# Laying out score operands by DMA instead of by 0/1 matmuls in a four-layer kernel on one Trainium2 core

## What is computed

```python
# layer 0: attention with rotary positions, 16 heads of 8, then a mixture of experts (2 of 8)
# layer 1: attention with a latent of 32 for keys and values, rotary, 16 heads of 8, then a channel mix
# layer 2: attention with sigmoid scores, 16 heads of 8, then a mixture of experts (2 of 8)
# layer 3: linear attention, then an MLP
scores = q @ k.T * 8 ** -0.5          # per head, causal
out = softmax(scores) @ v             # layer 2: sigmoid in place of softmax
```

## Time and profile before

| | |
|---|---|
| runs | 1676.58, 1678.48, 1684.9 us; median 1678.48 us |
| profiled execution | time 1675.6 us, span 1673.8 us from first to last instruction, mean granted TensorE clock 0.925 |
| busy in the span | PE 1430.4 us, DVE 1011.3 us, ACT 726.8 us, POOL 252.6 us |
| stages by the trace | rope attention to about 404 us, routed experts to about 590 us, latent attention to about 984 us, channel mix to about 1045 us, sigmoid attention to about 1272 us, the rest to the end |

### The profile page before, as it was taken

One profiled execution on the slowest core, in us unless ns is written; L12 is line 12 of the kernel. 1 busy time (PEld: TensorE's weight loads), 2 busy tenths in 40 slices (PEclk: granted clock), 3 DMA queues, 4 the chain that ended last, 5 costly groups with the idle time before them and its releaser, 6 DMA issues.

```text
span 1673.8 us, 33692 instructions
## 1 busy us (share of the span) xinstructions
PE 1430.4 (85%) x12538; PEld 1083.1 (65%) x12538; DVE 1011.3 (60%) x2801; ACT 726.8 (43%) x1281; POOL 252.6 (15%) x514
## 2 busy tenths in 40 slices
PE   5999999997069489999999965799996999998987
PEld 3666666664059456666666644466665999997667
DVE  4677777674336347777777649344444666664856
ACT  0444434442246324445444433467664555543322
POOL 0000000000521312222221013000000000001433
PEclk7999999996579769999999979699998999998989
DMA  9100000000022200000000000000000000000001
GB/s 301 31 2 1 1 1 2 2 1 1 34 60 71 96 4 5 8 8 8 8 5 5 2 0 2 1 2 2 2 1 1 1 2 2 1 2 1 1 17 35
DMA packets 32673, 30.39 MB, mean 18 GB/s; under 512 B 4536, under 2 KB 29312, under 8 KB 31872
## 3 DMA queue, kind: packets, MB, share of 16 engines
q1 hardware_dynamic: 30464, 24.05, 4.6%
q0 software_dynamic: 2048, 4.20, 0.8%
HBM read 18.01 MB, written 10.22 MB: 17 GB/s over the span
## 4 chain that ended last, share of the span: by engine, by line
PE 71%; DVE 12%; ACT 5%; issue 4%; POOL 4%; DMA 2%; SPq 0%; POOLq 0%; DVEq 0%; ACTq 0%
PE S L355 12%; PE O L1559 7%; PE O L425 6%; PE S L341 5%; PE A L329 4%; PE S L344 4%; PE A L310 3%; ACT probs L647 3%; PE A L330 3%; PE O L429 3%; PE S L1541 2%; DVE nm L826 2%; PE A L446 2%; PE O L2105 2%; PE S L1542 2%
## 5 line engine op out<-in xcount | busy, mean ns | idle before, releaser
L647 ACT ACTIVATE probs<-S 128x1024 f32<-128x1024 f32 x288 | 289.4, 1025 | 170.3 <-PE S L355 161.7
L823 DVE TENSOR_REDUCE nm<-S 128x4 f32<-128x1024 f32 x128 | 151.7, 1214 | 71.5 <-PE S L355 71.2
L156 POOL TENSOR_TENSOR ve<-mv,eps 128x2 f32<-128x2 f32 x112 | 26.3, 235 | 1075.4 <-DVE mv L148 1075.4
L1627 ACT ACTIVATE probs<-S,eb 128x256 f32<-128x256 f32 x256 | 107.5, 473 | 118.1 <-PE S L1543 118.1
L1559 PE MATMUL O<-ew,probs 128*128 128x128 f32 x1024 | 138.2, 278 | 0.3 <-ACT probs L1627 0.2
L654 ACT COPY OT<-O 128x512 f32<-128x512 f32 x96 | 56.2, 585 | 180.5 <-PE O L429 180.5
L1559 PEld LDWEIGHTS O<-ew,probs 128*128 128x128 f32 x1024 | 125.2, 192 | 5.1 <-ACT probs L1627 3.5
L425 PE MATMUL O<-probs,V 128*32 128x256 f32 x1536 | 123.1, 393 | 4.7 <-ACT probs L647 3.4
L329 PE MATMUL A<-hi,spread 128*128 128x256 f32 x384 | 108.0, 314 | 21.5 <-DVE lo L802 8.8
L167 DVE TENSOR_SCALAR X<-res,mv,rstd 128x128 f32<-128x128 f32 x224 | 85.4, 422 | 66.4 <-POOL rstd L160 65.9
L355 PEld LDWEIGHTS S<-KS,QS 32*128 32x128 f32 x1024 | 74.4, 192 | 57.3 <-issue 57.3
(11 more groups left out here) (341 smaller groups left out, 3065.3 us busy)
## 6 DMA issues: line engine op xcount, KB each, us to landing
ew<-in_w SPq DMA_DIRECT2D x2, 2048.0 KB, 10.2
moe_rows<-zeros SPq DMA_DIRECT2D x1, 2944.0 KB, 13.6
xin<-moe_rows SPq DMA_DIRECT2D x23, 128.0 KB, 2.5
ew<-in_w SPq DMA_DIRECT2D x2, 1024.0 KB
out<-X SPq DMA_DIRECT2D x16, 128.0 KB, 1.8
moe_made<-ctx_sb SPq DMA_DIRECT2D x12, 128.0 KB, 1.8
moe_made<-ctxT SPq DMA_DIRECT2D x11, 128.0 KB, 1.8
probs<-in_spread SPq DMA_DIRECT2D x1, 1024.0 KB, 5.2
```

The costliest lines, as they stand in the source:

```text
L647: act.activation(c.probs[:, n].rearrange("p b g l -> p b (g l)"), c.S[:, n % 2], ACT.Exp if soft else ACT.Tanh, scale=self.scale).then_inc ...
L823: dve.tensor_reduce(c.nm[:, 1, 2 * pr:2 * pr + 2, 2 * u:2 * u + 2], slot.rearrange("p b (g k) -> p b g k", g=2), AX.X, ALU.max, negate=Tru ...
L1627: act.activation(w["h"][:, x % 2, j], c.S[:, x % 2, bank, col:col + L], ACT.Relu, bias=w["b1"][:, x * self.NJ + j:x * self.NJ + j + 1]).th ...
```

## The change

The stacks on PE and both copies are taken out of all three attentions. In their place SP, after a wait for `hi` and then for `lo`, issues 24 DMAs per sequence from SBUF to SBUF, each 32 partitions by 256 numbers (32 KB): channel rows of one group go to every fourth partition of `QS` or `KS`. The strip's row order changes accordingly (`MAX_HI`, `MAX_LO`). Two semaphores, `stk0` and `stk1`, count the landings for groups 0, 1 and groups 2, 3. `QS` is zeroed and `KS` filled with the ones once at the start and once again behind the routed experts, which use the same memory. Weight loads that stood at the start are spread over the steps of the rope and latent attentions, behind the 24 DMAs of a sequence, and the load of `spread` is gone.

```diff
-MAX_HI = 3 * HD
-MAX_LO = MAX_HI + 1
+SLOTS = ROWS // HD
+MAX_HI = SLOTS - 1
+MAX_LO = 2 * SLOTS - 1
...
+    def fill_stacks(self, dve, filled):
+
+        dve.memset(self.QS[:].bitcast(F32), 0.0).then_inc(filled, 1)
+        dve.tensor_copy(self.KS[:].rearrange("p n g l -> p (n g l)"), self.one_rows[:].broadcast_to((P, 2 * G * L))).then_inc(filled, 1)
...
+    def sync(self, sp, others):
+        c, e = self.c, self.e
+        stacks = [c.QS[:].bitcast(F32), c.KS[:].bitcast(F32)]
+        halves = [e["stk0"], e["stk1"]]
+
+        def spread(par, part, j, slot, half):
+            for g in (2 * half, 2 * half + 1):
+                sp.dma_start(stacks[j][slot:P:SLOTS, par, g, :], part[ROWS * g:ROWS * (g + 1), j, :].bitcast(F32))\
+                  .then_inc(halves[half].sem, 16)
+
+        for s in range(B):
+            par = s % 2
+            sp.wait_ge(e["hi"].sem, e["hi"].at(s))
+            if begun(s - 2):
+                sp.wait_ge(e["p2"].sem, e["p2"].at(s - 2))
+            for half in range(2):
+                spread(par, c.hi, 0, 0, half)
+                spread(par, c.hi, 0, 1, half)
+                spread(par, c.hi, 1, 0, half)
+                spread(par, c.hi, 1, 2, half)
+            sp.wait_ge(e["lo"].sem, e["lo"].at(s))
+            for half in range(2):
+                spread(par, c.lo, 0, 2, half)
+                spread(par, c.lo, 1, 1, half)
+            others(s)
...
         def x_transposes(s, par):
-            if begun(s - 1):
-                pe.wait_ge(e["ks"].sem, e["ks"].at(s - 1))
+            if soft:
+                if begun(s - 1):
+                    pe.wait_ge(e["t12"].sem, e["t12"].at(s - 1))
+            elif begun(s - 3):
+                pe.wait_ge(e["ctx"].sem, e["ctx"].at(s - 3))
...
         def pass1(s, par, n):
 
-            if n == 0:
-                pe.wait_ge(e["qs"].sem, e["qs"].at(s))
-                pe.wait_ge(e["ks"].sem, e["ks"].at(s))
             if n < 2:
+                stacked = e["stk1" if n else "stk0"]
+                pe.wait_ge(stacked.sem, stacked.at(s))
...
             pass2(k, par, 3)
-            if has_front:
-                stack(k + 1, 0)
             weighted(k, par, 0, has_front)
             pass2(k, par, 4)
-            if has_front:
-                stack(k + 1, 1)
             pass2(k, par, 5)
...
         def round_hi(s):
             act.wait_ge(e["rot"].sem, e["rot"].at(s))
             if begun(s - 1):
-                act.wait_ge(e["kst_ps"].sem, e["kst_ps"].at(s - 1))
+                act.wait_ge(e["stk0"].sem, e["stk0"].at(s - 1))
+                act.wait_ge(e["stk1"].sem, e["stk1"].at(s - 1))
             act.copy(c.hi[:], c.rot[:]).then_inc(e["hi"].sem, 1)
```

More of the change, by code:

```diff
@@ L391, in pass2 @@
                 pe.wait_ge(e["qm"].sem, e["qm"].at(s, n + 1))
[L392 to L395, removed]
+            if n < 2 and not soft:
+                stacked = e["stk1" if n else "stk0"]
+                pe.wait_ge(stacked.sem, stacked.at(s))
             if n >= 2:
@@ L798, in round_lo @@
             if begun(s - 1):
-                dve.wait_ge(e["kst_ps"].sem, e["kst_ps"].at(s - 1))
+                dve.wait_ge(e["stk0"].sem, e["stk0"].at(s - 1))
+                dve.wait_ge(e["stk1"].sem, e["stk1"].at(s - 1))
             if not soft:
@@ L2227, in dve @@
         finish(self.NT - 1)
+        c.fill_stacks(dve, c.refilled)
         for q in range(self.FIRST):
@@ L2346, in build @@
         load("moe2", second["gate"][:], d["gate_2"])
-        load("moe2", second["w1"], d["w1_2"])
-        load("moe2", second["w2"], d["w2_2"])
+        for k in range(0, NE, 2):
+            load("moe2", second["w1"][:, k:k + 2], d["w1_2"][:, k:k + 2])
+            load("moe2", second["w2"][:, nj2 * k:nj2 * (k + 2)], d["w2_2"][:, nj2 * k:nj2 * (k + 2)])
         load("moe2", second["b1"][:], d["b1_2"])
@@ L2374, in build @@
         rope.after, latent.before = experts0, experts0
-        experts0.loaded = loaded["moe0"], 16 * len(loads["moe0"])
-        N_MADE = 31
+        experts0.loaded = loaded["l0"], 16 * len(loads["l0"])
+        N_MADE = 32
         def fold_products(pe):
@@ L2420, in _, with beside_rope, beside_latent @@
         def _(sp):
-            for group in ("consts", "l0", "x0", "x", "moe0", "l1", "l2", "l3"):
+            for group in ("consts", "l0", "x0", "x"):
                 for dst, src in loads[group]:
                     sp.dma_start(dst, src).then_inc(loaded[group], 16)
-            rows = phases[1][1].rows
             sp.wait_ge(made, N_MADE)
-            sp.dma_start(rows.rearrange("(n p) d -> p n d", p=P),
-                         routed["zeros"][:].unsqueeze(1).broadcast_to((P, rows.shape[0] // P, P))).then_inc(zeroed, 16)
+            rows = phases[1][1].rows.rearrange("(n p) d -> p n d", p=P)
+            early = [(group, *pair) for group in ("moe0", "l1", "l2", "l3") for pair in loads[group]]
+            late = [("moe2", *pair) for pair in loads["moe2"]]
+            def beside_rope(s):
+                for group, dst, src in early[3 * s:3 * s + 3] if s < B - 1 else early[3 * s:]:
+                    sp.dma_start(dst, src).then_inc(loaded[group], 16)
+                if s < ZEROINGS:
+                    n = rows.shape[1] // ZEROINGS
+                    sp.dma_start(rows[:, s * n:(s + 1) * n],
+                                 routed["zeros"][:].unsqueeze(1).broadcast_to((P, n, P))).then_inc(zeroed, 16)
+            def beside_latent(s):
+                for group, dst, src in late[s:s + 1] if s < B - 1 else late[s:]:
+                    sp.dma_start(dst, src).then_inc(loaded[group], 16)
+            rope.sync(sp, beside_rope)
             experts0.sync(sp)
@@ L2430, in _ @@
             sp.wait_ge(experts0.s["bias"], 2 * experts0.NT)
-            for dst, src in loads["moe2"]:
-                sp.dma_start(dst, src).then_inc(loaded["moe2"], 16)
+            sp.wait_ge(c.refilled, 2)
+            latent.sync(sp, beside_latent)
+            phases[4][1].sync(sp, lambda s: None)
             phases[-1][1].sync(sp)
```

66 lines of the change are left out of this document (15 added, 51 removed).

## The result

The changed kernel takes 2149.91 us (median of 4 runs, 2145.45 to 2156.37) against 1679.26 us (4 runs on the same chip, 1676.58 to 1684.9): 1.2801 times as long, 95% interval 1.2770 to 1.2831. The forecast was 1980 us, range 1850 to 2150. The direction was as forecast, and so was the mechanism; the size was 170 us short.

What follows compares the result with a forecast made beforehand. PE's own work was taken to bound the kernel before; DMA waits and clock loss add +113 us in rope, +107 in latent, +72 in sigmoid, which with smaller terms makes +304 on 1675.6: 1980 us, range 1850 to 2150.

Steps and rivals of the forecast that it cites:

- The bound and the way of reading: Attention steps, read in time order: PE-bound before; afterwards score slots wait for DMAs, 11.0 to 12.9 us behind hi.
- Spacing 0.47 us, bounds 0.40 to 0.51: SP's queue behind each hi: time between starts of successive DMA issues, 24 per sequence, taken from loads in the trace.
- Landing 2.0 us: Each new DMA: 2.0 us from the start of its issue until its data has landed in SBUF.
- The clock: PE's clock falls in every stall, returns 4.4 us into `weighted`; costs 2.3 us per rope or latent step, 1.9 in sigmoid.
- clock stays up: Rival: PE's clock does not fall in the stalls, or only now and then; 1876 us, chance 0.17.
- Comes back late: Rival: PE's clock returns only with the projections, 7.2 us lost instead of 2.3 in 32 steps; 2137 us, chance 0.15.
- Last steps, start and gather: Outside the loops: sixteenth sequences' waits +20 us, less loaded at the start -3.4, earlier rows behind routed experts 4.8 saved.
- The transfers hide: Rival: SP's issues cost nothing, only bytes count, so transfers fit beside PE's work; 1569 us, chance 0.05.

Runs made afterwards that it cites:

- hi alone: Changed kernel without the 8 DMAs of the remainders (lo) per sequence, leaving 16: 1895.18 us (one execution).
- five forms: Kernel before, with bursts of 12 unread DMAs on SP in seven forms, varying stride, size and SBUF or HBM as source or destination: 1685.41 us.
- The two queues: Changed kernel with ACT issuing the 8 DMAs of hi into `KS` and SP the other 16: 1947.54 us, 1.1604 times the kernel before.
- the versions through HBM: Changed kernel with hi and lo stored to HBM and loaded back by six or three loads, in several variants: 1831.41, 1790.75, 1800.6 and 1780.43 us.
- the control: Kernel before, stacks by matmul, with only the weight loads spread over the steps and the zeroing in two parts: 1680.4 us, 1.0006.
- direct pairs: Changed kernel with 12 SBUF to SBUF DMAs of 64 KB per sequence (9 SP, 3 POOL), `weighted(k, 1)` moved ahead, 10 filler matmuls: 1718.03 us, 1.0193.
- through HBM, `weighted` first: Changed kernel with hi and lo stored to HBM, six loads back, and `weighted(k, 1)` ahead of `pass1(k+1, 0)` in rope and latent: 1790.75 us, 1.0677.

## Why the prediction was right, and where its size was off

*The bound and the way of reading.* Right: score slots that wait for DMA, with all of the next step queued behind them. hi alone confirms it, since 8 issues taken off the queue gave 4.9 us per step back. The two queues gained as much (5.0 us per rope step), but ended on another path, through ACT's issues and exponentials.

*Spacing 0.47 us, bounds 0.40 to 0.51: the step that failed.* It measured 0.637 on SP, in all five forms from SBUF to SBUF, and 0.66 on ACT, outside the bounds. I took the price from single loads and a group of four, none with this spread of rows. Coming from HBM does not by itself make a load cheaper, since loads from HBM with the change's spread cost 0.64 too. The term of the sum is 23 (or 19) spacings per sequence: 23 x 0.167 = 3.8 us in 32 steps and 19 x 0.167 = 3.2 us in 16, +173 us, and 1980 + 173 = 2153 against 2150 measured. That this closes so well is in part luck, since the errors below cancel, and so is it that 2149.91 lies inside a range that ended at 2150: two of the four executions lie above it, and the room at the top had been left for a clock that comes back late, not for this spacing.

*Landing 2.0 us.* 1.9 measured.

*The clock.* Fall and return as forecast, the return 3.0 instead of 4.4 us into `weighted`. From the second slot to the next hi 17.3 us against 15.4, so 1.9 us per step where 2.3 stood; in sigmoid 6.4 us (1464.22 to 1470.66) against 4.8, 1.6 where 1.9 stood. The rival "clock stays up" did not happen. "Comes back late" happened in one latent step of the changed kernel (5 us, shown above), and in many steps of the versions through HBM.

*Last steps, start and gather.* Outside the three loops the span grew by 31 us; the sum had 12. Most of what was missed lies between the last hi of rope and the first of latent, 237.3 us against 224.4, +13 where the sum had +3. The first hi came 1.8 us earlier (3.4 said). Behind the routed experts the gain was 2.2 us (4.8 said), 4.84 us from 741.84 to 746.68 against the 7.08 of the earlier trace rows; the first of POOL's DMAs took twice as long as usual:
```profile
741.84 1.99 POOL L1926 DMA_INDIRECT yt<-moe_made,sli  x1 [6.44 <-DMA moe_made<-ctx_sb]
...
746.68 0.42 DVE L1943 TENSOR_TENSOR X<-X,yt 128x256 f32<-128x256 f32 x1 [3.72 <-DMA yt<-moe_made,sli]
```
In the control the moved loads gained nothing that could be told from no change. These terms were small and partly wrong, and their errors stand against the lesser clock loss.

*The transfers hide.* Excluded: it needed a spacing of 0.23 us. The run with 12 DMAs shows what it takes, a release by 7.4 us behind hi in every step; it had that in some steps, and over the whole kernel nothing of PE's 99 us was gained.

What stays open: why a wait of 1.11 us leaves the clock up in one kernel and one of 1.12 us is followed by 12 us at 1.2 GHz in another, and whether direct pairs in the old order of `weighted` would beat the kernel before; that was not tried.

## What to carry to other kernels

Count the DMA instructions on a queue before the bytes: here each cost 0.64 us of its engine from 16 to 128 KB, so 24 small ones per step were the critical path with the DMA engines under a quarter busy. A second queue takes its share only by holding up what its engine does behind it. Merge the instructions by laying source and destination out so that one instruction carries more, but check what the merging adds: a round trip through HBM cost two landings, and doubled stores came with full DMA engines. A matmul that only moves data also keeps PE busy; take it away, and a wait that opens in its place can be paid a second time through the clock, 1.9 us per rope step here.

## What the hardware showed that I had not expected

A DMA out of SBUF into SBUF occupied SP for 0.594 us in the median whatever its size between 16 and 128 KB (0.607 for the pairs, 0.619 on ACT, 0.564 on POOL), one to HBM for 0.37 to 0.42. The Trainium skill's advice to coalesce small transfers ("DMA: Bandwidth & Descriptors", section "Rules for kernel authors") agrees: 12 DMAs of 64 KB took 7.5 us of issue (5.82 on SP and 1.70 on POOL, side by side), 24 of 32 KB took 15.2.

POOL's indirect DMA took 1.99 us at 741.84, beside a CAST of 1.16 us on DVE that began at 741.80, and 0.94 to 1.02 elsewhere. In the control with only the moved loads, which has no such CAST there, the same DMA took 1.00. The Trainium skill says in "SBUF — State Buffer", section "SBUF: two separate sides", that GpSimd cannot write descriptors while VectorE runs an operation in a two-port mode, such as a float32 copy from SBUF to SBUF. The two rows agree with that; whether this CAST runs in such a mode no run here shows.

With short waits of PE the granted clock went both ways in the same kernel (through HBM, `weighted` first): steps of 23 and of 31 us stood side by side with the same instructions, about 7 of the 8 us between them made by the clock (20 us at 1.2 GHz in the one and 3.4 in the other, an estimate with the prediction's factor of 1.69 for work at the low clock).
